# Conv, linear attention and expert layer on one core: low halves and router tie products moved off VectorE, transposed fp32 split from PSUM and replicated by DMA, and a new program order for every engine

## The reference

```python
x = x + _L0_conv_ref(_gn(x), gamma, beta, W)     # batch norm, signs of x and of W, 3x3 convolution
t = _to_tokens(x)                                # 3136 tokens of 32 channels an image
t = t + _L1_attn_ref(_ln_t(t), ...)              # 16 heads of width 32
t = t + _L1_ffn_ref(_ln_t(t), ...)               # 8 experts, the best 2 of a token
```

```python
denom = 1.0 / (einsum(q_cos, k_cos.sum(axis=1)) + einsum(q_sin, k_sin.sum(axis=1)) + 1e-05)
o = qkv * denom[..., None]
return o.reshape(b, s, h * d) @ dense_w.T + dense_b
```

## Time and profile before

| | us |
|---|---|
| median of 3 runs | 2692.53 |
| lowest and highest run | 2686.22 and 2696.71 |
| span of the profiled execution (its first to its last instruction) | 2691.5 |
| time of the profiled execution itself | not listed apart; it stands 1 us from the median by its span |
| PE busy | 2363.6 (88%) |
| DVE busy | 2278.2 (85%) |
| POOL busy | 1865.1 (69%) |
| ACT busy | 1743.1 (65%) |

### The profile page before, as it was taken

How to read it: one execution, slowest core, us unless ns; L and a number is a source line. 1 busy time by engine, 2 the same in 40 slices (tenths; PEclk the granted TensorE clock), 3 DMA queues, 4 the chain that set the end, 5 groups by cost and what they waited for, 6 DMA issues and landing times.

```text
span 2691.5 us, 57490 instructions
## 1 busy us (share of the span) xinstructions
PE 2363.6 (88%) x19300; PEld 1162.4 (43%) x19300; DVE 2278.2 (85%) x2849; ACT 1743.1 (65%) x2821; POOL 1865.1 (69%) x1479
## 2 busy tenths in 40 slices
PE   3479999999999999998999999899898999999972
PEld 3324444444444444444444444444444444444442
DVE  4457999898998989898898989999898989999973
ACT  0167777676776767666776767777676767777630
POOL 0124777777777777776777777777777777777677
PEclk7589999999999999999999999999999999999995
DMA  9200000000000000000000000000000000000000
GB/s 261 34 13 10 11 16 17 10 8 17 17 17 17 17 17 5 14 17 17 17 16 17 6 12 17 17 17 16 18 12 7 16 17 17 17 11 7 7 7 12
DMA packets 235817, 55.16 MB, mean 20 GB/s; under 512 B 229648, under 2 KB 230528, under 8 KB 235360
## 3 DMA queue, kind: packets, MB, share of 16 engines
q1 hardware_dynamic: 235488, 50.96, 9.4%
HBM read 31.19 MB, written 12.85 MB: 16 GB/s over the span
## 4 chain that ended last, share of the span: by engine, by line
PE 41%; DVE 32%; issue 17%; ACT 5%; POOL 2%; DMA 1%; DVEq 1%; SPq 1%; ACTq 0%; POOLq 0%
PE ps L606 7%; DVE kbuf L987 7%; PE ps L581 6%; DVE qbuf L993 5%; PE ps L572 4%; PE ps L623 4%; PE ps L597 3%; PE ps L564 3%; DVE route L1052 3%; PE ps L657 3%; PE ps L632 3%; DVE prod L1077 2%; DVE rs L1010 2%; ACT ebuf L717 2%; PE ps L645 2%
## 5 line engine op out<-in xcount | busy, mean ns | idle before, releaser
L712 ACT ACTIVATE ebuf<-ps,small 112x1024 f32<-112x1024 f32 x448 | 498.5, 1113 | 279.0 <-PE ps L572 242.0
L987 DVE SCALAR_TENSOR_TENSOR kbuf<-ps,ebuf 112x1024 f32<-112x1024 f32 x448 | 542.7, 1211 | 113.1 <-ACT ebuf L712 110.1
L811 POOL TENSOR_TENSOR qbuf<-spread_r,qbuf 128x896 f32<-128x896 f32 x224 | 473.9, 2116 | 179.4 <-ACT spread_r L747 179.3
L993 DVE SCALAR_TENSOR_TENSOR qbuf<-ps,ebuf 128x896 f32<-128x896 f32 x448 | 485.8, 1084 | 84.5 <-ACT ebuf L717 62.6
L717 ACT ACTIVATE ebuf<-ps,small 128x896 f32<-128x896 f32 x448 | 451.4, 1008 | 122.8 <-PE ps L597 71.1
L581 PE MATMUL ps<-kbuf,xcs 112*64 112x512 f32 x1792 | 488.8, 624 | 39.1 <-issue 32.7
L789 POOL TENSOR_TENSOR rstd<-varr,power 112x28 f32<-112x28 f32 x64 | 307.2, 4800 | 183.1 <-DVE varr L977 179.5
L632 PE MATMUL ps<-qbuf,gmat 128*64 128x224 f32 x3584 | 387.5, 358 | 39.4 <-DVE pbuf L1021 35.9
L840 POOL TENSOR_TENSOR prod<-prod 112x512 f32<-112x512 f32 x224 | 285.7, 1276 | 103.0 <-DVE prod L1077 103.0
L747 ACT ACTIVATE spread_r<-ps 128x896 f32<-128x896 f32 x224 | 205.5, 917 | 171.1 <-PE ps L623 162.0
L632 PEld LDWEIGHTS ps<-qbuf,gmat 128*64 128x64 f32 x3584 | 237.0, 137 | 157.0 <-DVE pbuf L1021 44.0
(11 more groups left out here) (133 smaller groups left out, 3530.2 us busy)
## 6 DMA issues: line engine op xcount, KB each, us to landing
qbuf<-in_x SPq DMA_DIRECT2D x8, 1568.0 KB, 11.6
xt<-in_x SPq DMA_DIRECT2D x256, 49.0 KB
out<-ffn SPq DMA_DIRECT2D x256, 49.0 KB
shifted<-nat SPq DMA_DIRECT2D x128, 52.6 KB, 5.0
qbuf<-in_sel SPq DMA_DIRECT2D x1, 1024.0 KB, 11.8
tabn<-in_tabnc SPq DMA_DIRECT2D x1, 784.0 KB, 13.5
p<-in_p2c SPq DMA_DIRECT2D x1, 528.0 KB, 10.4
tabd<-in_tabdc SPq DMA_DIRECT2D x1, 448.0 KB, 11.0
```

What stands on the lines that cost most here:

```text
L712: act.activation(ebuf[0:PT, 0, :].rearrange("p (a b) -> p a b", a=2), o[0:PT, :, :], ACT.Exp, bias=minus_one[0:PT, :]).then_inc(kexp_made, 1)
L811: nc.gpsimd.tensor_tensor(qbuf[:, 2:4, n, :], spread_r[:, :, :], qbuf[:, 2:4, n, :], ALU.mult)\
L987: v.scalar_tensor_tensor(kbuf[:, n % 2, :].rearrange("p (a b) -> p a b", a=2), o[0:PT, :, :], 1.0, ebuf[0:PT, 0, :].rearrange("p (a b) -> ...
L993: v.scalar_tensor_tensor(qbuf[:, k0:k0 + 2, j, :], o[:, :, 0:G * PT], 1.0, ebuf[:, 1, 0:2 * G * PT].rearrange("p (a b) -> p a b", a=2), AL ...
```

## The change

1. **Low halves.** ZT and ZU become 7 fp32 transposes of xn, two to four to a PSUM bank. ACT copies the result to fp16 (`zhl[:, 0]`, the high half, 128 channels of 4 slots), DVE writes PSUM minus the high half to `zhl[:, 1]`. SP then copies the halves to the four row groups of z1 or z2 by 16 DMAs of 32 x 784 fp16 (50 KB each). XH1, XH2, PL1 and PL2 are gone.
2. **Reciprocal.** RL (den minus its fp16 copy) goes from DVE, two instructions of 64 x 224, to POOL, one of 128 x 448 a part. ACT's two copies of 64 x 224 read `r_high` in place of `den` and stand in a step of their own, RH, that waits for RL.
3. **Router.** The logits are read in PSUM by DVE's first maximum and comparison, and ACT copies them to SBUF (LG). The product of the candidates with their ranks (`first`) goes from DVE to POOL (RF, two an image).
4. **Order.** `SCHEDULE` and `SHIFTS` become one table of positions for each engine, `ORDER`.

```diff
-    add("ZT", [-6.30, -2.45])
-    add("ZU", [32.28, 32.83])
...
+ORDER = {
+    "tensor": {
+        "K": [-4.06, -3.18, -2.48, -1.95, -0.56, -0.23, 0.27, 2.13, 2.71, 3.20, 3.58, 4.69, 5.33, 6.62],
...
@@ sync
+                if kind in ("ZT", "ZU") and n == 0:
+                    ln = kind == "ZU"
+                    sp.wait_ge(zlow_made[ln], m.at(2, 2))
+                    for r in range(4):
+                        for g in range(G):
+                            dst = z2[32 * r:32 * r + 32, g] if ln else z1[32 * r:32 * r + 32, m.par, g]
+                            sp.dma_start(dst.rearrange("p j t -> p (j t)"),
+                                         zhl[ln][32 * g:32 * g + 32, r % 2, :]).then_inc(z_in[ln], 16)
@@ tensor
-                    pe.wait_ge(parts_made[ln], m.at(1, 1))
-                    pe.wait_ge(eye16_made, 1)
...
+                    pe.wait_ge(xn_made[ln], m.at(1, 1))
+                    for j in range(4 * n, 4 * n + HALF[n]):
+                        mm = pe.transpose(o[:, 0, PT * (j % 4):PT * (j % 4) + PT],
+                                          xn[ln][:, 4 * j:4 * j + 4, :].rearrange("p s c -> p (s c)"), eye[0:PT, 0:PT])
...
-                    pe.wait_ge(z_made[0], m.at(2, n // 7 + 1))
+                    pe.wait_ge(z_in[0], m.at(256, 256))
...
-                    pe.wait_ge(z_made[1], m.at(2, 2))
+                    pe.wait_ge(z_in[1], m.at(256, 256))
@@ scalar
-                    act.activation(dst.rearrange("p (a b) -> p a b", a=2), o.bitcast(F16)[:, :, 0:7 * PT], ACT.Copy)\
-                        .then_inc(z_made[ln], 1)
+                    wait(act, z_in[ln], m.at(256))
+                    a, b = COL[n]
+                    act.activation(zhl[ln][:, 0, a:b], o[:, 0, 0:b - a], ACT.Copy).then_inc(high_made[ln], 1)
...
+                elif kind == "RH":
+                    act.wait_ge(r_made, m.at(2, n + 1))
                     for c in range(2):
-                        last = act.activation(rs[0:64, n, HALFW * c:HALFW * (c + 1)], den[64 * c:64 * c + 64, 0:HALFW],
-                                              ACT.Copy)
+                        last = act.activation(rs[64 - 64 * c:128 - 64 * c, n, HALFW * c:HALFW * (c + 1)],
+                                              r_high[64 * c:64 * c + 64, :], ACT.Copy)
...
+                elif kind == "LG":
+                    act.wait_ge(route_step, m.at(13, 2))
+                    act.activation(route[:, 0, :], o[0:PT, 0, 0:SLOTS * EXPERTS], ACT.Copy).then_inc(logits_kept, 1)
@@ gpsimd
-                elif kind in ("PL1", "PL2"):
...
+                elif kind == "RL":
+                    pool.wait_ge(rhigh_made, m.at(2, n + 1))
+                    both = [128, 2, HALFW]
+                    nc.gpsimd.tensor_tensor(rs[:, n, :].rearrange("p (c t) -> p c t", c=2),
+                                            den[:, 0:HALFW].unsqueeze(1).to_broadcast(both),
+                                            r_high[:, :].unsqueeze(1).to_broadcast(both), ALU.subtract).then_inc(r_made, 1)
+                elif kind == "RF":
+                    pool.wait_ge(route_step, m.at(13, 2 if n == 0 else 7))
+                    hot = route[:, 1 + n, :]
+                    nc.gpsimd.tensor_tensor(hot, hot, first[:, :], ALU.mult).then_inc(hot_ranked, 1)
@@ vector
+                elif kind in ("ZT", "ZU"):
+                    ln = kind == "ZU"
+                    dve.wait_ge(high_made[ln], m.at(2, n + 1))
+                    a, b = COL[n]
+                    v.tensor_tensor(zhl[ln][:, 1, a:b], o[:, 0, 0:b - a], zhl[ln][:, 0, a:b], ALU.subtract)                        .then_inc(zlow_made[ln], 1)
...
-                elif kind == "RL":
-                    dve.wait_ge(rhigh_made, m.at(2, n + 1))
...
-                        v.tensor_tensor(hot, hot, first[:, :], ALU.mult).then_inc(route_step, 1)
+                        dve.wait_ge(hot_ranked, m.at(2, 1 if n == 0 else 2))
```

More of the change, by code:

```diff
@@ L198, in iteration @@
 def iteration(engine, i):
-    shift = SHIFTS[engine]
-    steps = sorted((t + shift.get(kind, 0), t, kind, n) for t, kind, n in SCHEDULE)
     out = []
-    for t, t0, kind, n in steps:
-        d = int(t // PERIOD)
-        out.append((t - PERIOD * d, t0, kind, i - d, n))
-    return [(kind, m, n) for _, _, kind, m, n in sorted(out) if 0 <= m < B]
+    for kind, times in ORDER[engine].items():
+        for n, t in enumerate(times):
+            d = int(t // PERIOD)
+            out.append((t - PERIOD * d, kind, i - d, n))
+    return [(kind, m, n) for _, kind, m, n in sorted(out) if 0 <= m < B]
 ITERATIONS = range(-3, B + 3)
@@ L367, in build @@
         pe_pre = sem("pe_pre")
-        eye16_made = sem("eye16_made")
         dve_pre = sem("dve_pre")
@@ L1005, in step @@
                     v.reciprocal(den[:, 0:HALFW], den[:, 0:HALFW]).then_inc(recip_made, 1)
-                elif kind == "RL":
-                    dve.wait_ge(rhigh_made, m.at(2, n + 1))
-                    for c in range(2):
-                        q = slice(64 * c, 64 * c + 64)
-                        last = v.tensor_tensor(rs[64:128, n, HALFW * c:HALFW * (c + 1)], den[q, 0:HALFW], r_high[q, :],
-                                               ALU.subtract)
-                    last.then_inc(r_made, 1)
                 elif kind == "R":
@@ new lines, in step @@
+                        v.tensor_reduce(top1, src, AX_X, ALU.max).then_inc(route_step, 1)
+                        after(1)
+                        v.tensor_tensor(grid(hot1), src, spread(top1), ALU.is_equal).then_inc(route_step, 1)
+                    elif n in (0, 3):
+                        hot, w = (hot1, w1) if n == 0 else (hot2, w2)
+                        dve.wait_ge(hot_ranked, m.at(2, 1 if n == 0 else 2))
+                        v.tensor_reduce(w, grid(hot), AX_X, ALU.max).then_inc(route_step, 1)
+                    elif n == 1:
+                        after(3)
+                        v.tensor_tensor(grid(hot1), grid(hot1), spread(w1), ALU.is_equal).then_inc(route_step, 1)
+                        dve.wait_ge(logits_kept, m.at(1, 1))
+                        after(4)
+                        v.scalar_tensor_tensor(rest, hot1, -3.0e38, logits, ALU.mult, ALU.add).then_inc(route_step, 1)
@@ L1055, in step @@
                     elif n == 2:
                         after(5)
-                        v.tensor_tensor(grid(hot1), grid(hot1), spread(w1), ALU.is_equal).then_inc(route_step, 1)
+                        v.tensor_reduce(top2, grid(rest), AX_X, ALU.max).then_inc(route_step, 1)
                         after(6)
-                        v.scalar_tensor_tensor(rest, hot1, -3.0e38, logits, ALU.mult, ALU.add).then_inc(route_step, 1)
-                    elif n == 5:
-                        after(11)
+                        v.tensor_tensor(grid(hot2), grid(rest), spread(top2), ALU.is_equal).then_inc(route_step, 1)
+                    elif n == 4:
+                        after(8)
@@ L1068, in step @@
                         v.reciprocal(w2, w1).then_inc(route_step, 1)
-                        after(15)
+                        after(12)
                         v.tensor_tensor(w1, ratio, w2, ALU.mult).then_inc(route_step, 1)
```

140 lines of the change are left out of this document (48 added, 92 removed), and 57 rows, old and new, of tables (ORDER, SHIFTS).

## The result

The changed kernel takes 2613.95 us (median of 4 runs, 2610.9 to 2619.01) against 2691.34 us of the kernel before on the same chip: a ratio of 0.972, with a 95% interval of 0.970 to 0.975. The forecast was 2593 us, so the kernel came out 21 us slower than forecast.

A forecast was written before the change was run, and what follows sets the result against it. PE and DVE, both over 90% busy, bound the kernel, each at times waiting for the other. From the 2691.5 us span, 32 x 3.5 off and 13 added for the ends gave 2592.5, forecast 2593 us; range 2525 to 2700.

The forecast's parts named there:

- The engines' sums: Busy time an image: PE net -1.9 us, DVE net -4.2, ACT -3.4 or more, POOL -0.7.
- What it gives on the path: Image gain between PE's 1.9 us and the chain's 4.9; 3.5 taken, middle of 4.1 and 2.9, leaving 72.5 us.
- the rival of the full relief: DVE was the real bound and its relief counts fully: 4.9 us an image, 2549 us; chance 0.22.
- the signs of being wrong: Profile signs: PE waiting on z's DMA, DVE's maximum on POOL's product, or PE and DVE both idler without such releasers.
- DVE is no longer level with PE: Undisturbed image of 72.5 us: PE 69.6 us, 96% busy, DVE 65.4; DVE's gain stops being worth its 4.2.
- The port question with them: DVE's tie products L1052 wait for the SBUF port shared with POOL; moving them gains the whole 2.4 us an image.
- 32 x 3.5 - 13: Whole-run gain: 3.5 us for each of 32 images, less 13 us for late first K and last logits.
- The replication: SP's copies from ZU's transposes to the logits, some 12 to 14 us, just fit behind 13.8 us of PE work.
- late halves: Rival: PE waits at the logits for a 20.7 us copy path, +3.4 us an image, 2814 us; chance 0.14.
- The sign that I gave: Profile after: K (L572) and logits (L651) on PE with next to no idle time released by a DMA.
- POOL late: Rival: DVE's router maximum waits for POOL's RF, losing 3 to 4 us an image, around 2700 us; chance 0.09.
- The branch: Loop's branch image took 81.2 us, PE idle 3.17 us, then slow matmuls; the change has no part in it.

The follow-up runs named there:

- the late RL: RL moved from POOL back to DVE in its old two-instruction form, at about its old position (11.50), against the changed kernel: 2750.61 us.

## Why the prediction came out as it did

**The engines' sums held.** PE -69 us (forecast 61), DVE -138 (134). The transposes were taken at 70 us and are 58.7.

**The steady image held as a number: 3.47 us gained, 3.5 forecast; 72.07 us with PE 96% busy where nothing is late, 72.5 and 96% forecast.** But the step "What it gives on the path" made it from operations alone, as pieces of the chain that go and come, and this is not where it comes from. The same operations in the old order cost 180 us in all, and the new order is worth 258. By 24 steady images it is 77.8 us an image before, 82.3 with the new operations in the old order (1976.3 us for the 24), and 74.4 with both. So the operations cost 4.5 us where the prediction had a gain of 3.5, and the order gave 7.9 where it had nothing: I used the new order to hide the copies, named it in the rival of the full relief and among the signs of being wrong, and gave it no term. The number agrees because two errors of 8 us each cancel, and that is luck. How large each is depends on my placing of the new steps in the old order. The chain's pieces were those of the old order, and a forecast for a new one can't be added up from them.

**That DVE is no longer level with PE was half right.** An undisturbed image has no use for 1.8 us less of DVE, and about half of what is added to PE shows. But RL back on DVE at a good place still costs 29 us, so DVE is not free either. The chain goes through PE, DVE, POOL and ACT, which speaks for a cycle over all four; that it sets the 72 us is not shown, and which of its links is the longest was not settled.

**The port.** "The port question with them" failed. The product left DVE, but the wait of 2 us stayed and met L1064, which now stands beside POOL's multiplication: 63.2 us in all, of which 57 are waiting. Of the 2.4 us an image that I counted as gain, only 0.8 was the products' own work (half of the 64 took 0.39 us or less). By the Trainium skill (GPSIMD Engine Reference, Architecture) the port to SBUF is shared by the two engines; the trace agrees, since the wait went away when the instruction moved (1974 to 180 ns), and does not depend on its size. At that place it hardly mattered for the time, 9 us; with the products back on DVE such a wait stands ahead of R, and matters.

**The images at the ends: the term that was mis-sized.** The sum took 32 x 3.5 - 13. The 24 steady images gave their 83.4 us; the remaining 8 images less the ends were forecast at +15 and came to -6, and this is the whole error of 21 us. The 13 was nearly right: the first product with `tabd` comes 7.75 us later than before (203.69 against 195.94; PE waits 13.02 and 4.73 us for the first copies), and from the last one to the end it takes 7.3 us more (128.55 against 121.25), 15 in all. Wrong was the gain of 3.5 us for every one of the other images, 28 us. The four behind the first product gain 8.0 together and those behind the steady part 1.1. In an emptying pipeline less and less work covers the 14 us path; these are the last two images' logits:

```profile
2520.07 2.75 PE L651 MATMUL ps<-we,z 128*112 128x8 f16 x28 [8.97 <-DMA z<-zhl]
2576.26 2.75 PE L651 MATMUL ps<-we,z 128*112 128x8 f16 x28 [12.59 <-DMA z<-zhl]
```

Half of the copies gave 34 us, 25 of them at the two ends.

**The replication.** Forecast 12 to 14 us of path against 13.8 of work; measured 1.6 (evictions) + 10.1 (16 issues) + 1.9 (landing) = 13.6 us against 13.2 from the end of the transposes to the logits. The parts were off in opposite directions: an issue is 0.59 us, near the upper bound, and a landing is 1.9 us, under the lower bound of 3.3 that I took from copies of short pieces. The rival "late halves" did set in, in a small way that I had not priced: logits that wait 0.5 to 0.8 us cost 2 us each, in six of 24 images, since the lower clock comes on top. The run with 28 copies shows its slope, 0.6 us for each copy beyond 16, with the clock's share in it. The sign that I gave, next to no idle time released by a DMA, came out at 17.8 us for K and 28.9 for the logits, 42 of these 46.7 in the first and last images. The Trainium skill (DMA: Bandwidth & Descriptors, Anatomy of one DMA) gives a fixed 2.0 us for a DMA that GpSimd issues. SP issues these, and the trace's landing of 1.9 us is close to it.

**POOL late.** Not in this order (7.7 us in all), true in the old one (62.0).

**The branch** was left out as untouched. It nearly is: its images take 75.7 us on average in the steady part against 72.0 undisturbed, where it was 80.0 against 75.7, and 13 branches are now the cheapest thing to remove.

## What to carry to other kernels

When a change moves work and order together, price them apart: a chain read from the old order gives the worth of an operation only in that order, and here the same operations lose 180 us in one order and gain 77 in another. Ask of each moved or added step what stands behind it in its engine's queue and how much time lies until its first reader. Where it came in time it cost little here; where it came late, PE waited, and the waits were often paid again in slow matmuls. A path that just fits in the median image is late in some of them, so leave it room. Count the ends of a pipeline with their full latency, and the images there with little gain (9 us in place of 28).

## What the runs showed of the hardware

- Three kinds of DVE instructions with both operands in SBUF that met POOL's multiplication lasted until about its end: 28 elements a partition took 2.08 us beside a multiplication of 2.28, and 0.18 away from it; a comparison of 224 elements took 1.82 for 0.39; a product of 224 took 2.20 for 0.39. A maximum over 224 elements, with one operand, took its usual 0.39 us beside such a multiplication (1151.56, in the run with the tie products back).
- A copy from SBUF to SBUF of 32 rows of 1568 bytes takes SP 0.59 us to issue (0.63 between starts) and 1.9 us to land; SP's 16 issues took 10.1 us, five times the landing, and 11.0 where the logits were late.
- Waits of PE are often paid twice. Idle times of 2.67 and 3.86 us were followed by stretches at the lower clock (L581 1.91 us for 1.01, L632 3.25 for 1.66); of the 137 us that the late RL cost, 54 are busy time of PE for the same matmuls. Behind the wait of 2.02 us (tie products back) the matmul took its usual 0.55, and the next four of L581 1.08. But behind a wait of only 0.50 us at the logits L581 took 1.80 for 1.08, so the length of the wait alone does not tell.
